# Two weight tensors laid out ahead of four work tensors in SBUF, in a two-layer graph kernel

## The chip, the cores and the metric

The kernel runs on one core of one Trainium2 chip. The metric is the device time of one execution, in microseconds (us); lower is better. The time before is the median of three runs.

## The reference

128 graphs of 128 nodes with 256 features go through two layers. The first is a layer norm, a ReLU, a linear layer and a product with a weighted adjacency matrix, with a residual. The second is a layer norm, a ReLU, graph attention with 8 heads, an output projection, a sigmoid and a residual.

```python
h = jnp.maximum(_layernorm(x, axis=-1), 0.0)
x = x + (adj @ (h @ L0_weight) + L0_bias)
h = jnp.maximum(_layernorm(x, axis=-1), 0.0)
feat_proj = (h @ fc_w + fc_b)                  # 8 heads of 256 columns
logits = feat_proj @ q_w + q_b + swap(feat_proj @ k_w + k_b)
attn = softmax(leaky_relu(logits + (1.0 - adj) * NEG, 0.01))
out = concat_heads(attn @ feat_proj) @ fp_w + fp_b + h
x = x + sigmoid(out)
```

All data is float32.

## The kernel before

Nodes lie on the 128 partitions. Two graphs make a pair (`j` is 0 or 1 in it), and there are 64 pairs. The kernel first multiplies each head's `fc_w` by its rows of `fp_w`, so that one 256 by 256 matrix per head is left; the eight are kept as `m_hi` and `m_lo`, the rounded values and what the rounding left over (`fold`, with its matmuls on line 417). Precision is kept in the whole kernel in this way: an operand is split in a high and a low part of type float32r, and `split` (line 396) makes a product of three matmuls, low by high, high by low and high by high.

For each pair, TensorE does this. A matmul has a stationary operand, which a weight load brings into the array, and a moving operand, which streams through it.

- `aggregate` (line 442): adjacency by features, float32, with `h0_f` stationary and `g_in` moving. In the profile: `bank<-g_in,h_f`.
- `transform`: `ah_hi`, `ah_lo` stationary, the first layer's weights `w0_hi`, `w0_lo` moving, 256 columns. In the profile: `bank<-w_hi,ah_lo` and the like.
- `transpose_h` (line 465), and `queries_keys` (line 478) with `u` stationary and `hT_hi`, `hT_lo` moving, 256 columns.
- `project`, 8 calls of 6 matmuls: `hT_hi`, `hT_lo` stationary, `m_hi`, `m_lo` moving, 512 columns. In the profile: `gbank<-m_hi,hT_lo` and the like. ScalarE copies each bank to `g_hi[j]` (line 1249), and VectorE subtracts that from the bank to give `g_lo[j]` (line 830).
- `transpose_p` (line 497), after which ScalarE and VectorE write `pT_hi[j]` (line 1263) and `pT_lo[j]` (line 837).
- `attend`, 4 calls of 12 matmuls: `pT_hi[j]`, `pT_lo[j]` stationary, `g_hi[j]`, `g_lo[j]` moving, 256 columns. In the profile: `ybank<-g_hi,pT_lo` and the like.

The work of neighbouring pairs overlaps. The order of the work on each of the five engines is written out by hand: a beginning, a loop whose body `step` handles one pair (57 passes on TensorE), and an end. Semaphores join the engines.

What the change touches is the allocation of SBUF at the head of `gnn_pair`. `sb(name, shape, dt, align)` takes the next free bytes of every partition, from the next multiple of `align`; `two(...)` makes two tensors, one for each `j`. `LINE` is 64 bytes and `SPAN` 256. `ah`, `hT`, `pT`, `fcb` and `m` are placed at multiples of `SPAN`, `w0`, `g` and `u` at multiples of `LINE`. `fcb` is 64 bytes long. A row of `m` is `MROW` = 576 elements, and `project` reads its 512 columns from element `MAT` = 16, so 64 bytes into the row. The loops, the semaphores and the tensors' sizes say nothing of addresses.

Of the kernel before, what the change touches and what calls it, by code (L numbers as in the profile page):

```python
# [6 lines left out]
F32R = mybir.dt.float32r  # L7
# [3 lines left out]
P = 128  # L11
D = 256
DT = D // P
# [16 lines left out]
SPAN = 256  # L30


HP = H // 2
MAT = LINE // 4
MROW = 2 * D + 64
# [15 lines left out]
def gnn_pair(nc, graph, identity, head_mask, row_coef, w0, bias0, fc_wT, fc_b, qk_w, q_b, k_b, fp_w, fp_b, out):  # L51
# [9 lines left out]
    with ExitStack() as ctx:  # L61
        def sb(name, shape, dt=F32, align=32):
            return ctx.enter_context(nc.sbuf_tensor(name, shape, dt, align_bytes=align))
# [7 lines left out]
        def two(name, shape, dt=F32, align=32):  # L71

            return [sb(f"{name}{k}", shape, dt, align) for k in range(J)]
# [13 lines left out]

        fcb = sb("fcb", [P, H * DT], F32, SPAN)
        w0_hi, w0_lo = sb("w0_hi", [P, DT, D], F32R, LINE), sb("w0_lo", [P, DT, D], F32R, LINE)
        g_hi, g_lo = two("g_hi", [P, H * D], F32R, LINE), two("g_lo", [P, H * D], F32R, LINE)  # L90

        u = sb("u", [P, DT, 2 * HALF], F32R, LINE)
        m_hi, m_lo = sb("m_hi", [P, DT, HP, MROW], F32R, SPAN), sb("m_lo", [P, DT, HP, MROW], F32R, SPAN)


        ident = sb("ident", [P, P])
# [1793 lines left out]
```

How the kernel before makes its waits and increments, by code:

```python
            def load(p, q):  # L253
                if has(p - U):
                    sp.wait_ge(a_h0f, 2 * (p - U + 1))
                    sp.wait_ge(pe_ah, p - U + 1)
                    sp.wait_ge(g_xb, p - U + 1)
                    sp.wait_ge(g_t, p - U + 1)
                if has(p - 1):
                    sp.wait_ge(s_loaded, 16 * (p + 1) - 16)
                sp.dma_start(g_in[q][:], graph[p]).then_inc(s_loaded, 16)
# [1 line left out]
            def store(p):  # L263
                sp.wait_ge(g_res, p + 1)
                sp.dma_start(out[p].rearrange("n (j d) -> n j d", j=J), res).then_inc(s_stored, 16)
# [1 line left out]
            def keys_out(p, q):  # L267
                sp.wait_ge(v_kq, p + 1)
                if has(p - 1):
                    sp.wait_ge(s_rows, 16 * p)
                sp.dma_start(key_rows[q][0:HALF + ROWS], kq_sb[q][0:HALF + ROWS]).then_inc(s_rows, 16)
# [1 line left out]
            def queries_in(p, q):  # L273
                sp.wait_ge(s_rows, 16 * (p + 1))
                if has(p - 1):
                    sp.wait_ge(s_queries[0], 16 * p)
                    sp.wait_ge(s_queries[1], 16 * p)
                if has(p - U):
                    for n in range(J * NC):
                        sp.wait_ge(v_mx[n], p - U + 1)
                for j in range(J):
                    rows = key_rows[q][j * HALF + H:j * HALF + ROWS].rearrange("h n -> n h")
                    sp.dma_start(qs[q][:, j, :], rows, allow_slow_non_contiguous=True).then_inc(s_queries[j], 16)
```

## Time and profile before

| | |
|---|---|
| median of three runs | 1412.72 us (1412.06 to 1412.76) |
| profiled execution, its own time | 1412.72 us |
| its span, first to last instruction | 1410.8 us |
| granted TensorE clock, mean over the span | 0.999 |
| TensorE matmul busy | 1400.5 us, 99% |
| weight load busy | 1258.8 us, 89% |
| VectorE / ScalarE / GpSimd busy | 1286.0 / 1125.6 / 1102.2 us |

The span leaves out 1.9 us of the profiled execution's time. Busy time of TensorE is not a measure of its pace here: matmuls are pipelined, their ends are modelled, and one that is shown with 0.28 us is followed by the next after 0.11 us. The pace is read from the starts in the timeline.

### The profile page before, as it was taken

To read this page: it belongs to the slowest core of one execution; us is meant where nothing else is said; L and a number is where in the kernel's file an instruction comes from. 1 tells how busy PE (TensorE), PEld (TensorE's weight loads), DVE (VectorE), ACT (ScalarE), POOL (GpSimd) and SP (SyncE) were. 2 spreads that over 40 slices of the span, in tenths; PEclk is the share of its full clock that TensorE was granted. 3 is DMA by queue.
4 is the path that set the end of the run, shared out by engine and by line. 5 is a ranking of instruction groups with operands and counts; after the bars stand their busy time and mean duration, and the time that the engine had idled before them with its cause. 6 is when DMAs were issued, how large, how long until landed. Compare 5 with 4: busy or idle time off the path is not lost.

```text
span 1410.8 us, 31568 instructions
## 1 busy us (share of the span) xinstructions
PE 1400.5 (99%) x9048; PEld 1258.8 (89%) x9048; DVE 1286.0 (91%) x4396; ACT 1125.6 (80%) x3417; POOL 1102.2 (78%) x1297
## 2 busy tenths in 40 slices
PE   9999999999999999999999999999999999999998
PEld 7888999899899899998998998998989989988987
DVE  7999999999999999999999999999999999998996
ACT  4878788788888888887887888888878878887876
POOL 5787877878778878778787787787787877878764
PEclk9999999999999999999999999999999999999999
DMA  7323323323223233233132232232331332322321
GB/s 240 94 63 107 107 54 105 95 65 105 78 81 106 58 101 106 54 105 100 59 105 82 77 106 61 98 106 54 105 103 56 105 85 74 106 66 85 76 58 42
DMA packets 177131, 124.68 MB, mean 88 GB/s; under 512 B 137808, under 2 KB 143568, under 8 KB 177104
## 3 DMA queue, kind: packets, MB, share of 16 engines
q1 hardware_dynamic: 176816, 124.35, 30.4%
q8 instruction: 12, 0.20, 0.1%
q14 instruction: 15, 0.12, 0.0%
q10 hardware_dynamic: 288, 0.01, 0.0%
HBM read 105.98 MB, written 18.35 MB: 88 GB/s over the span
## 4 chain that ended last, share of the span: by engine, by line
PE 94%; POOL 2%; DMA 1%; issue 1%; DVE 1%; SPq 0%; ACT 0%; POOLq 0%
PE gbank L396 48%; PE ybank L396 24%; PE tbank L497 8%; PE bank L396 6%; PE bank L442 4%; PE bank L478 2%; PE bank L465 2%; DMA late<-fc_wT_dram 1%; PE gbank L417 1%; DMA late<-key_rows 0%; POOL att L1587 0%; POOL att L1580 0%; DVE att L847 0%; POOL ends L1603 0%; DVE att L854 0%
## 5 line engine op out<-in xcount | busy, mean ns | idle before, releaser
L1256 ACT ACTIVATE att<-att 128x128 f32<-128x128 f32 x1024 | 397.8, 393 | 43.3 <-DVE att L854 39.2
L1580 POOL TENSOR_TENSOR att<-late,t_pos 128x512 f32<-128x512 f32 x256 | 330.6, 1293 | 127.9 <-PE tbank L497 122.7
L396 PE MATMUL gbank<-m_hi,hT_lo 128*128 128x512 f32 x1024 | 428.0, 418 | 0.0
L396 PE MATMUL gbank<-m_hi,hT_hi 128*128 128x512 f32 x1024 | 402.0, 393 | 0.0
L396 PE MATMUL gbank<-m_lo,hT_hi 128*128 128x512 f32 x1024 | 401.5, 392 | 0.0
L830 DVE TENSOR_TENSOR g_lo<-gbank,g_hi 128x512 fp32r<-128x512 f32 x512 | 341.5, 679 | 47.5 <-ACT g_hi L1249 42.9
L1587 POOL TENSOR_TENSOR att<-att,rinv 128x512 f32<-128x512 f32 x256 | 288.9, 1129 | 106.8 <-DVE rinv L859 106.4
L1249 ACT ACTIVATE g_hi<-gbank 128x512 fp32r<-128x512 f32 x512 | 290.6, 594 | 42.5 <-PE gbank L396 42.2
L847 DVE TENSOR_SCALAR_CACHE_REDUCE att<-att,qs 128x128 f32<-128x128 f32 x1024 | 291.7, 341 | 30.4 <-POOL att L1580 30.1
L396 PE MATMUL ybank<-g_hi,pT_lo 128*128 128x256 f32 x1016 | 283.2, 279 | 0.0
L396 PE MATMUL ybank<-g_hi,pT_hi 128*128 128x256 f32 x1016 | 283.0, 279 | 0.0
L396 PE MATMUL ybank<-g_lo,pT_hi 128*128 128x256 f32 x1016 | 282.5, 278 | 0.0
L1263 ACT ACTIVATE pT_hi<-tbank 128x512 fp32r<-128x512 f32 x256 | 152.9, 597 | 149.0 <-PE tbank L497 144.1
L396 PEld LDWEIGHTS gbank<-m_hi,hT_hi 128*128 128x128 f32 x1024 | 192.2, 188 | 43.3
L396 PEld LDWEIGHTS gbank<-m_lo,hT_hi 128*128 128x128 f32 x1024 | 193.7, 189 | 25.1
L396 PEld LDWEIGHTS gbank<-m_hi,hT_lo 128*128 128x128 f32 x1024 | 192.9, 188 | 25.5
L396 PEld LDWEIGHTS ybank<-g_lo,pT_hi 128*128 128x128 f32 x1016 | 190.8, 188 | 10.4
L396 PEld LDWEIGHTS ybank<-g_hi,pT_lo 128*128 128x128 f32 x1016 | 190.9, 188 | 9.9 <-DVE pT_lo L837 0.2
L1256 ACT ACTIVATION_READ_ACCUMULATOR att<-att 128x1 f32 x1024 | 194.8, 190 | 0.0
L854 DVE SCALAR_TENSOR_TENSOR att<-att 128x516 f32<-128x516 f32 x256 | 193.8, 775 | 0.2
L396 PEld LDWEIGHTS ybank<-g_hi,pT_hi 128*128 128x128 f32 x1016 | 190.5, 187 | 0.0
L837 DVE TENSOR_TENSOR pT_lo<-tbank,pT_hi 128x512 fp32r<-128x512 f32 x256 | 173.7, 678 | 5.3 <-ACT pT_hi L1263 4.3
(97 smaller groups left out, 2317.9 us busy)
## 6 DMA issues: line engine op xcount, KB each, us to landing
late<-key_rows SPq DMA_DIRECT2D x64, 1024.0 KB, 6.1
g_in<-graph_dram SPq DMA_DIRECT2D x64, 512.0 KB, 3.4
out_dram<-ends SPq DMA_DIRECT2D x63, 256.0 KB, 3.8
qs<-key_rows SPq DMA_DIRECT2D x128, 4.0 KB, 2.4
key_rows<-kq_sb SPq DMA_DIRECT2D x64, 24.0 KB, 1.4
att<-fc_wT_dram SPq DMA_DIRECT2D x4, 256.0 KB, 5.7
late<-fp_w_dram SPq DMA_DIRECT2D x4, 256.0 KB, 5.3
ends<-fp_w_dram SPq DMA_DIRECT2D x2, 512.0 KB, 7.8
```

The costliest lines, as they stand in the source:

```text
L396: mm = pe.matmul(out_ap, w, m, start=first and n == 0, stop=last and n == len(terms) - 1)
L442: mm = pe.matmul(sums[:, j, dt, :], h0_f[q][:, j, dt * P:(dt + 1) * P], adjT_of(q)[:, j, :], start=True, stop=True)
L497: mm = pe.transpose(tbank[:, h * P:(h + 1) * P], att[j][c][:, h * P:(h + 1) * P], ident[:])
L830: dve.tensor_tensor(g_lo[j][:, s], bank[:], g_hi[j][:, s].bitcast(F32), ALU.subtract)\
L837: dve.tensor_tensor(pT_lo[j][:, hs, :], rows, pT_hi[j][:, hs, :].bitcast(F32), ALU.subtract)\
L847: r = dve.tensor_scalar(a[:, s], a[:, s], qs[q][:, j, c * HC + h:c * HC + h + 1], None, ALU.add, ALU.min, accum_out=a[:, CH + h:CH + h + 1])
L854: dve.scalar_tensor_tensor(out=a, in0=a, scalar=SLOPE, in1=a, op0=ALU.mult, op1=ALU.min)\
L1249: act.activation(g_hi[j][:, s], gbank[tenant(RING, RSIZE, n, p)[0]][:], ACT.Copy).then_inc(a_g[n], 1)
L1256: e = act.activation(a[:, s], a[:, s], ACT.Exp, scale=-1.0, bias=a[:, CH + h:CH + h + 1], accum_out=esum[j][c][:, h:h + 1])
L1263: act.activation(pT_hi[j][:, c * HC:(c + 1) * HC, :], rows, ACT.Copy).then_inc(a_pT[NC * j + c], 1)
L1580: gp.tensor_tensor(a, keys[q][:, j, c * HC:(c + 1) * HC, :], t_pos[q][:, j, :].unsqueeze(1).broadcast_to([P, HC, P]), ALU.add)\
L1587: gp.tensor_tensor(a, a, rinv[j][c][:].unsqueeze(2).broadcast_to([P, HC, P]), ALU.mult)\
```

## The change

The line that allocates `m_hi` and `m_lo` moves up, from behind `u` to before `g_hi` and `g_lo`. Nothing else is changed.

```diff
@@ -87,10 +87,10 @@
 
         fcb = sb("fcb", [P, H * DT], F32, SPAN)
         w0_hi, w0_lo = sb("w0_hi", [P, DT, D], F32R, LINE), sb("w0_lo", [P, DT, D], F32R, LINE)
+        m_hi, m_lo = sb("m_hi", [P, DT, HP, MROW], F32R, SPAN), sb("m_lo", [P, DT, HP, MROW], F32R, SPAN)
         g_hi, g_lo = two("g_hi", [P, H * D], F32R, LINE), two("g_lo", [P, H * D], F32R, LINE)
 
         u = sb("u", [P, DT, 2 * HALF], F32R, LINE)
-        m_hi, m_lo = sb("m_hi", [P, DT, HP, MROW], F32R, SPAN), sb("m_lo", [P, DT, HP, MROW], F32R, SPAN)
```

Each engine executes the same instructions in the same order, with the same waits. The addresses follow from the sizes and alignments; the first aligned tensor starts at byte 16640 of a partition.

| tensor | start before | mod 256 | start after | mod 256 |
|---|---|---|---|---|
| `pT_hi0`, `pT_hi1`, `pT_lo0`, `pT_lo1` | 41216, 45312, 49408, 53504 | 0 | the same | 0 |
| `w0_hi`, `w0_lo` | 57664, 59712 | 64 | the same | 64 |
| `g_hi0`, `g_hi1` | 61760, 69952 | 64 | 98816, 107008 | 0 |
| `g_lo0`, `g_lo1` | 78144, 86336 | 64 | 115200, 123392 | 0 |
| `u` | 94528 | 64 | 131584 | 0 |
| `m_hi`, `m_lo` | 95232, 113664 | 0 | 61952, 80384 | 0 |
| `ident`, and all behind it | 132096 | 0 | the same | 0 |

The 192 bytes that padding takes ahead of `m_hi` are taken in both kernels, so nothing behind `m` or `u` moves. The columns of `m` that `project` reads start at 64 mod 256 in both. `hT` and `ah` lie at 0 mod 256 and stay where they are.

## Rows read from the trace of the kernel before

**Rows 1.** The page: span, TensorE's busy time and granted clock in 40 slices, the chain by engine.
```profile
span 1410.8 us, 31568 instructions
...
PE 1400.5 (99%) x9048; PEld 1258.8 (89%) x9048; DVE 1286.0 (91%) x4396; ACT 1125.6 (80%) x3417; POOL 1102.2 (78%) x1297
...
PEclk9999999999999999999999999999999999999999
...
PE 94%; POOL 2%; DMA 1%; issue 1%; DVE 1%; SPq 0%; ACT 0%; POOLq 0%
```
**Rows 2.** Waits of TensorE in 60:1350: line, waited for: us, times, longest.
```profile
PE bank L465 <- ACT h L1233: 0.8, 1, 0.8
PE tbank L497 <- POOL att L1587: 0.5, 1, 0.5
```
**Rows 3.** The chain that ended last: start us, length us; one place, two passes.
```profile
707.54 2.76 PE gbank L396 x12
729.07 2.76 PE gbank L396 x12
```
**Rows 4.** Timeline of TensorE, `attend` with `g1`, `pT1`: start us, us.
```profile
702.84 0.28 PE L396 MATMUL ybank<-g_hi,pT_lo 128*128 128x256 f32 x1
702.95 0.28 PE L396 MATMUL ybank<-g_lo,pT_hi 128*128 128x256 f32 x1
...
704.20 0.39 PE L396 MATMUL gbank<-m_hi,hT_lo 128*128 128x512 f32 x1
```
**Rows 5.** The same, `attend` with `g0`, `pT0`.
```profile
713.33 0.28 PE L396 MATMUL ybank<-g_hi,pT_lo 128*128 128x256 f32 x1
713.45 0.28 PE L396 MATMUL ybank<-g_lo,pT_hi 128*128 128x256 f32 x1
...
714.75 1.06 PE L442 MATMUL bank<-g_in,h_f 128*128 128x128 f32 x8
715.64 0.60 PE L497 MATMUL tbank<-ident,att 128*128 128x128 f32 x4
```
**Rows 6.** The same, one early `attend` with `g0`, `pT0`: first and last start.
```profile
113.59 0.28 PE L396 MATMUL ybank<-g_hi,pT_lo 128*128 128x256 f32 x1
...
114.84 0.28 PE L396 MATMUL ybank<-g_hi,pT_hi 128*128 128x256 f32 x1
```
**Rows 7.** The same, one early `attend` with `g1`, `pT1`: first and last start.
```profile
79.49 0.28 PE L396 MATMUL ybank<-g_hi,pT_lo 128*128 128x256 f32 x1
...
80.79 0.28 PE L396 MATMUL ybank<-g_hi,pT_hi 128*128 128x256 f32 x1
```
**Rows 8.** Timeline of TensorE, `queries_keys` of pair 0 and of a later pair.
```profile
27.56 0.28 PE L478 MATMUL bank<-hT_hi,u 128*64 128x256 f32 x1
27.67 0.28 PE L478 MATMUL bank<-hT_lo,u 128*64 128x256 f32 x1
27.78 0.28 PE L478 MATMUL bank<-hT_hi,u 128*64 128x256 f32 x1
...
700.99 0.28 PE L478 MATMUL bank<-hT_lo,u 128*64 128x256 f32 x1
701.46 0.39 PE L396 MATMUL gbank<-m_hi,hT_lo 128*128 128x512 f32 x1
```
**Rows 9.** Timeline of TensorE, 12 matmuls of `fold` in the beginning, and three of them.
```profile
11.32 2.78 PE L417 MATMUL gbank<-late,att 128*128 128x258 f32 x12
...
11.98 0.82 PE L417 MATMUL gbank<-late,att 128*128 128x258 f32 x3
```
**Rows 10.** Groups by line: shapes xcount | busy us, mean ns | idle before.
```profile
L830 DVE TENSOR_TENSOR g_lo<-gbank,g_hi 128x512 fp32r<-128x512 f32 x512 | 341.5, 679 | 47.5 <-ACT g_hi L1249 42.9
L837 DVE TENSOR_TENSOR pT_lo<-tbank,pT_hi 128x512 fp32r<-128x512 f32 x256 | 173.7, 678 | 5.3 <-ACT pT_hi L1263 4.3
L1249 ACT ACTIVATE g_hi<-gbank 128x512 fp32r<-128x512 f32 x512 | 290.6, 594 | 42.5 <-PE gbank L396 42.2
L1263 ACT ACTIVATE pT_hi<-tbank 128x512 fp32r<-128x512 f32 x256 | 152.9, 597 | 149.0 <-PE tbank L497 144.1
```
**Rows 11.** Busy time of the engines in the stretch 60:1350.
```profile
60.00:1350.00 1290.00, 1288.68 (x8373) 1160.44 (x8372) 1189.13 (x4072) 1045.00 (x3169) 1032.37 (x1198) 1.00 0.30 85
```

## The prediction

> **What bounds the kernel now.** I read four views in this order. The page comes first: TensorE is busy for 1400.5 of 1410.8 us, its clock is granted in full in every slice (2.4 GHz), and no other engine is above 91% [rows 1]. A busy share does not prove a bound, since the ends of matmuls are modelled. So the waits come second: between 60 and 1350 us, which is 91% of the span, TensorE's instructions waited for other engines twice, 1.3 us in all [rows 2]. The chain of waits says the same in another way: one place of the loop comes back after 729.07 - 707.54 = 21.53 us, and 94% of the chain is TensorE's [rows 1, 3]. The loop's 57 passes are then 57 x 21.53 = 1227 us, and their length is the sum of TensorE's own steps. The timeline comes last, because it shows those steps. What a reader is to see there is the distance between starts, not the duration.
>
> In an `attend` on the second graph, 12 matmuls of 256 columns take 704.20 - 702.84 = 1.36 us, 0.113 us each [rows 4]. In one on the first graph they take 714.75 - 713.33 = 1.42 us, 0.118 each [rows 5]. 256 columns at one per cycle of 2.4 GHz would be 0.107 us, so both are above the bare columns. Call the two paces quick and slow. Going through the starts of all 256 calls of `attend` in the trace, I count 121 quick (4 on `g0`, 117 on `g1`) and 135 slow (124 and 11).
>
> **The change part by part.** No instruction, wait or transfer is added, removed or reordered on any engine. What changes are addresses: `m` starts 33,280 bytes lower, and `g` and `u` start 37,056 bytes higher. So there are three things that could carry a time.
>
> *1. The residue of `g` under TensorE's reads.* `g` goes from 64 to 0 mod 256, and becomes equal there to `pT`, the weights loaded beside it. This concerns 256 x 12 = 3072 matmuls, and as nothing covers TensorE, each nanosecond on each of them is 3.1 us of the end. No float32r stretch of this trace has both operands at the same residue, so the cost has to be bounded.
> - If the pace hung on which addresses meet, `g0` and `g1` would differ always. They don't: the usually slow `g0` runs quick at 113.59, with 11 steps in 114.84 - 113.59 = 1.25 us, 0.114 each [rows 6], and the usually quick `g1` runs slow at 79.49, with 1.30 / 11 = 0.118 [rows 7]. Same tensors, same addresses, both paces. What differs is what stood ahead and how the stream came in. This is the strongest thing that the trace says for an address-free pace.
> - `queries_keys` has the mirrored residues, 0 moving and 64 stationary. In pair 0 its starts are 27.56, 27.67, 27.78, 0.11 apart: quick. Later its four take 701.46 - 700.99 = 0.47, 0.118 each: slow [rows 8]. The mirrored pair knows the same two paces.
> - Equal residues do occur in float32, at half the column rate. `aggregate` has both operands at 224 mod 256: its 8 records start over 715.64 - 714.75 = 0.89 us, 0.111 each, 0.0046 above the 256 cycles (0.1067) of its columns [rows 5]. `fold` has its weights at 96 and the moving operand at 32 to 240. The 12 records of [rows 9] have it at 72, 88, 96 and 112, four of them at 96, equal. The 12 cover 2.78 us; less the last one's 0.38 that is 2.40 / 11 = 0.218, 0.003 above the 516 cycles (0.215) of their columns, and the three that start at 11.98, of which the last two are equal ones, cover 0.82, so (0.82 - 0.38) / 2 = 0.22 each as well. No price of equality is seen there. `aggregate`'s excess over `fold`'s, 0.0046 - 0.003, less than 0.002 us for 512 bytes read, would be 0.004 for the 1024 bytes of a `g` matmul. I don't take it, since the two differ in shape too, but it is the upper end: 3072 x 0.004 = 12.3 us.
> - The lower end is that every slow call turns quick: 135 x (1.42 - 1.36) = 8.1 us gained.
> I take 0, by the nearest rows, [rows 6 to 8], which are the same type and the same width, and keep -8.1 and +12.3.
>
> The page "SBUF — State Buffer" of the Trainium skill, section "Who interferes with whom", gives TensorE two independent SBUF read ports, one for the moving operand and one for weight loads, and says that it never waits on anyone. By this rule the sum is 0 exactly. The trace agrees only in part: 0.113 and 0.118 against 0.107 show that something beside the columns costs time, and the rule does not name it, so it does not close the range.
>
> *2. The residue of `u`, and the absolute place of `m` and `g`.* `u` moves onto `hT`'s residue, in 4 x 64 = 256 matmuls. Between its two paces of 0.113 and 0.118 that is at most 256 x 0.005 = 1.3 us either way; I take 0. The columns read from `m` stay at 64 mod 256. Its row starts step by 2304 bytes and `g`'s by 1024 under `pT`'s 512, so the higher address bits already take many combinations inside one call, and the step within a call stays the same to 0.01 us [rows 4, 5]. A large boundary, such as 65536, already lies inside `g_hi0` before. I take 0 for the place.
>
> *3. The other engines' reads and writes of `g`.* VectorE writes `g_lo` at residue 64 in 679 ns and `pT_lo` at residue 0 in 678. ScalarE writes `g_hi` in 594 and `pT_hi` in 597 [rows 10]. So the residue is worth 3 ns at most. That is also off the path: VectorE is busy for 1189 of 1290 us in the steady stretch [rows 11], so it has about 100 us of room over some 480 writes of `g_lo` there, 0.2 us for each, before TensorE would have to wait for it. I take 0.
>
> The sum is 0. From the profiled execution: span 1410.8 + 0, with the 1.9 us that lie around it, gives 1412.7 us, which is also the median of the runs shown.
>
> **The rivals.**
> *Slower: equal residues lock `attend` into the slow pace.* The place is the moving read of `g` beside the load of `pT`. If reads that start on the same residue get in each other's way, the 121 quick calls become slow: 121 x 0.06 = 7.3 us, and the time is 1420.0. It decides from 1 ns a matmul upwards (3.1 us). For it: all float32r streams that are quick have the two operands at different residues, and `aggregate`, with equal ones, has a larger excess than `fold`. Against it: both paces on the same addresses [rows 6, 7], and equal residues at no price in `fold` [rows 9]. With the 0.004 of the upper end instead it would be 1425.0.
>
> *Faster: the slow calls turn quick.* The pace depends on how the stream before came in, so a small shift anywhere, an altered step in `queries_keys` or in `m`, can tip the calls on `g0`, 124 slow ones of 128, into the quick pace: up to 124 x 0.06 = 7.4 us with `g0` alone, 1405.3. For it: it needs only a nudge, and such calls exist [rows 6]. Against it: if addresses don't enter at all, nothing nudges, and the loop repeats as before.
>
> *The projection shifts instead.* `project` has 64 x 48 = 3072 matmuls of 512 columns. If its steps moved by 0.002 us on the average, that would be 6 us, to either side. Nothing in its residues changes, so this would have to be passed on from `attend`; I count it with the two above.
>
> **How the numbers follow.** A measurement of this kernel can tell about 0.2% from no change, 2.8 us. No effect of addresses, or one below that: 0.60. The slower rival, whole or in part: 0.25. The faster one: 0.15. The predicted time is that of the likeliest case, 1412.7. Its own range is 1411.5 to 1414. To leave out no more than 2 in 10 the range takes in the slower rival's 1420.0 and most of the faster rival: 1406 to 1420.5.
>
> **What would show it right or wrong.** Right: the place of [rows 3] still returns after 21.53 us, `attend` still has its 1.36 and 1.42 us calls in the same places, and the writes of `g` keep 679 and 594 ns. The slower rival shows as 1.42 us or more in `attend` on the second graph, with no wait of TensorE for another engine. The faster one shows as 1.36 us on the first graph. A wait of TensorE for VectorE's `g_lo` in the steady stretch would prove step 3 wrong. The forecast falls if a pass of the loop is longer or shorter than 21.53 by more than 0.05 us, for 57 of those are 2.8 us.

## The result, and the profile after

The changed kernel takes 1425.53 us (median, 1425.15 to 1426.06), the kernel before 1412.39 us in the same comparison. The ratio is 1.0094, with a 95% interval of 1.0077 to 1.0111: slower by 13.1 us. No change was forecast, and the time lies outside the stated range.

The page of the changed kernel, and the waits of TensorE in 60:1350, beside [rows 1] and [rows 2]:
```profile
span 1423.7 us, 31568 instructions
...
PE 1414.5 (99%) x9048; PEld 1271.2 (89%) x9048; DVE 1286.5 (90%) x4396; ACT 1124.1 (79%) x3417; POOL 1101.4 (77%) x1297
...
PEclk9999999999999999999999999999999999999999
```
```profile
PE tbank L497 <- POOL att L1587: 0.5, 1, 0.5
PE bank L465 <- ACT h L1233: 0.3, 1, 0.3
```
TensorE's clock is granted in full as before and it still waits for nobody (0.8 us). The busy times of the other engines are the same within 1.5 us. So the 12.9 us of span arise on TensorE itself. The chain of waits shows the length of a pass of the loop, as in [rows 3] (start us, length us):
```profile
496.30 2.76 PE gbank L396 x12
518.04 2.76 PE gbank L396 x12
```
A pass is now 21.74 us, 0.21 more than 21.53, and 57 x 0.21 = 12.0 of the 12.9 us. Note that the 12 `project` matmuls in the row still take 2.76 us. The timeline shows which ones don't. First a call of `attend` on `g1`, `pT1`, to be held against the 1.36 us of [rows 4]:
```profile
708.84 0.28 PE L396 MATMUL ybank<-g_hi,pT_lo 128*128 128x256 f32 x1
708.96 0.28 PE L396 MATMUL ybank<-g_lo,pT_hi 128*128 128x256 f32 x1
709.08 0.28 PE L396 MATMUL ybank<-g_hi,pT_hi 128*128 128x256 f32 x1
...
710.28 0.40 PE L396 MATMUL gbank<-m_hi,hT_lo 128*128 128x512 f32 x1
```
Then one on `g0`, `pT0`, to be held against the 1.42 us of [rows 5]:
```profile
719.50 0.28 PE L396 MATMUL ybank<-g_hi,pT_lo 128*128 128x256 f32 x1
...
720.94 0.27 PE L442 MATMUL bank<-g_in,h_f 128*128 128x128 f32 x1
```
Both take 1.44 us, 0.120 a matmul. The quick pace of 0.113 is gone, and what was slow (0.118) is a little slower. The groups by line show the same on their own scale. The modelled duration of a matmul of `attend` went from 279 to 283 ns, while that of `project` stays at 393, and the writes of `g` by VectorE and ScalarE stay where [rows 10] had them. First two groups of the kernel before, then the changed kernel:
```profile
L396 PE MATMUL gbank<-m_hi,hT_hi 128*128 128x512 f32 x1024 | 402.0, 393 | 0.0
...
L396 PE MATMUL ybank<-g_hi,pT_hi 128*128 128x256 f32 x1016 | 283.0, 279 | 0.0
```
```profile
L396 PE MATMUL gbank<-m_hi,hT_hi 128*128 128x512 f32 x1024 | 402.2, 393 | 0.0
L830 DVE TENSOR_TENSOR g_lo<-gbank,g_hi 128x512 fp32r<-128x512 f32 x512 | 341.4, 678 | 47.7 <-ACT g_hi L1249 43.0
L1249 ACT ACTIVATE g_hi<-gbank 128x512 fp32r<-128x512 f32 x512 | 290.6, 594 | 49.6 <-PE gbank L396 49.3
...
L396 PE MATMUL ybank<-g_hi,pT_hi 128*128 128x256 f32 x1016 | 287.8, 283 | 0.0
```

For the whole execution I summed the distances from each matmul's start to the next, by what it reads:

| us of the chain on TensorE | `attend` on g0 | `attend` on g1 | `project` | `transform` | `queries_keys` |
|---|---|---|---|---|---|
| before | 182.5 | 175.7 | 734.5 | 88.8 | 30.5 |
| after | 184.6 | 184.5 | 736.5 | 88.8 | 30.3 |
| difference | +2.1 | +8.8 | +2.0 | 0.0 | -0.2 |

### The profile page after: what moved, and what is told of

Its sections match the earlier page's. It is cut to its first block, busy times and chain, and to the rows that moved or that the text cites. A ratio compares the mean times of both kernels' runs of the same rounds, so it can differ in the third digit from the quotient of the medians.

```text
span 1423.7 us, 31568 instructions
## 1 busy us (share of the span) xinstructions
PE 1414.5 (99%) x9048; PEld 1271.2 (89%) x9048; DVE 1286.5 (90%) x4396; ACT 1124.1 (79%) x3417; POOL 1101.4 (77%) x1297
## 4 chain that ended last, share of the span: by engine, by line
PE 94%; POOL 2%; DVE 1%; issue 1%; DMA 1%; ACT 0%; POOLq 0%; SPq 0%; ACTq 0%
PE gbank L396 48%; PE ybank L396 25%; PE tbank L497 8%; PE bank L396 6%; PE bank L442 4%; PE bank L478 2%; PE bank L465 2%; DMA late<-key_rows 0%; POOL att L1587 0%; POOL att L1580 0%; DMA qk<-qk_w_dram 0%; PE gbank L417 0%; DVE att L847 0%; POOL xb L1570 0%; POOL t_pos L1572 0%
## 5 line engine op out<-in xcount | busy, mean ns | idle before, releaser
L396 PE MATMUL ybank<-g_hi,pT_hi 128*128 128x256 f32 x1016 | 287.8, 283 | 0.0
L396 PE MATMUL ybank<-g_lo,pT_hi 128*128 128x256 f32 x1016 | 287.3, 283 | 0.0
L396 PE MATMUL ybank<-g_hi,pT_lo 128*128 128x256 f32 x1016 | 287.2, 283 | 0.0
```

The source lines that it names most:

```text
L396: mm = pe.matmul(out_ap, w, m, start=first and n == 0, stop=last and n == len(terms) - 1)
```

## The experiments

The theory after the result: a float32r matmul is slower when its moving operand and the weights that are loaded beside it start at the same address mod 256 (the same residue). Rivals: the absolute place of `m` or `g` in the partition; a bad start at 0 mod 256 in itself; and `u`, which moved too. In what follows "distance" is the moving operand's start less the weights' start, mod 256. In every experiment each engine's instructions and waits are the same, in the same order; only addresses differ. Where a kernel says `ident` with `SPAN`, all that lies behind moves by 256 bytes or (in `e8_m_0`) not at all, so it keeps its residues.

**Place or residue.** `e1_place` is the changed kernel with 64 bytes ahead of `g`:
```diff
+        gap0 = sb("gap0", [P, 16], F32, LINE)
         g_hi, g_lo = two("g_hi", [P, H * D], F32R, LINE), two("g_lo", [P, H * D], F32R, LINE)
-        ident = sb("ident", [P, P])
+        ident = sb("ident", [P, P], F32, SPAN)
```


> m stays ahead of g as in the changed kernel, but g and u start 64 bytes later, so both are again at 64 mod 256; ident and all behind it move by 256 bytes, which keeps their residues. If the residue of g (or u) costs the 13 us, this is as fast as the kernel before: 1412 to 1414, with attend calls of 1.36 and 1.42 us. If the absolute place of m or g costs them, it stays at 1425, with calls of about 1.44 us.

Measured: 1412.82 us, ratio to before 1.0002 (0.9992 to 1.0012). With `m` ahead of `g`, but `g` back at 64, all of the loss is gone. Its call on `g1` in the timeline:
```profile
703.29 0.28 PE L396 MATMUL ybank<-g_hi,pT_lo 128*128 128x256 f32 x1
...
704.65 0.39 PE L396 MATMUL gbank<-m_hi,hT_lo 128*128 128x512 f32 x1
```
1.36 us, as in [rows 4]. `e2_g_u_0` is the reverse: the order of before, `m` on its old bytes, `g` and `u` at 0.
```diff
-        g_hi, g_lo = two("g_hi", [P, H * D], F32R, LINE), two("g_lo", [P, H * D], F32R, LINE)
+        g_hi, g_lo = two("g_hi", [P, H * D], F32R, SPAN), two("g_lo", [P, H * D], F32R, LINE)
```


> The order of before, m at its old bytes, g and u moved up by 192 bytes to 0 mod 256 into the padding ahead of m; nothing else moves. Residue theory: 1424 to 1427, attend calls of about 1.44 us. Place theory: 1412 to 1414.

Measured: 1424.63 us, ratio 1.0084 (1.0067 to 1.0101), a pass of 21.74 us. The loss is back without the move of `m`. The two together show that the place costs nothing and the residue all. `e1_place` also says something of the period: there `g` starts 320 bytes past `pT` mod 512, in the kernel before 64 bytes, and the time is the same.

**`g` or `u`.** `e3_u_0` gives `u` the alignment `SPAN` in the kernel before; `f0_g_0` puts `g` at 0 and keeps `u` at 64.
```diff
-        u = sb("u", [P, DT, 2 * HALF], F32R, LINE)
+        u = sb("u", [P, DT, 2 * HALF], F32R, SPAN)
```

> The kernel before with u alone at 0 mod 256 (moved up by 192 bytes); g, m and all else at their bytes. If only g's residue matters: 1412.4 within 1 us, attend unchanged. If u's share is what tips the pace of the whole loop: most of the 13 us.

> g alone at 0 mod 256, u kept at 64 (m and all behind it 256 bytes higher, residues kept). If g's equality with pT makes the whole of the 12 us: 1423 to 1426, attend near 120 ns in every call. If it needs u at 0 too: about 1420, since u alone gave 4.3 us.

Measured: `f0_g_0` 1426.1 us, ratio 1.0092 (1.0075 to 1.0108). A call on `g1` takes 1.44 us:
```profile
709.19 0.28 PE L396 MATMUL ybank<-g_hi,pT_lo 128*128 128x256 f32 x1
...
710.63 0.40 PE L396 MATMUL gbank<-m_hi,hT_lo 128*128 128x512 f32 x1
```
So `g` alone makes the whole loss, and `u` adds nothing to it. `e3_u_0` gave 1416.97 us, 1.0029 (1.0018 to 1.0041), where I had expected no change. Its own `queries_keys` got no slower (30.2 us against 30.5), although its operands are now at distance 0. So the theory does not hold for that stream, whose four matmuls at a time have only 64 columns of weights. But other calls changed their pace. On `g0` it is quick now (first two rows), on `g1` slow (last two):
```profile
716.12 0.28 PE L396 MATMUL ybank<-g_hi,pT_lo 128*128 128x256 f32 x1
...
717.49 0.27 PE L442 MATMUL bank<-g_in,h_f 128*128 128x128 f32 x1
```
```profile
705.47 0.28 PE L396 MATMUL ybank<-g_hi,pT_lo 128*128 128x256 f32 x1
...
706.88 0.40 PE L396 MATMUL gbank<-m_hi,hT_lo 128*128 128x512 f32 x1
```
1.37 us and 1.41 us. Summed over the execution: g0 -6.1, g1 +5.9, `transform` +2.8, `project` +1.6, which is +4.2 us.

**Equality, or a start at 0.** `e4_both_64` moves `pT` to 64, so that `g` and `pT` are equal at 64; `e5_mirror` has `pT` at 64 and `g` at 0 (`u` stands ahead of `g` in it, still at 64).
```diff
-        pT_hi, pT_lo = two("pT_hi", [P, H, P], F32R, SPAN), two("pT_lo", [P, H, P], F32R, SPAN)
+        gap0 = sb("gap0", [P, 16], F32, LINE)
+        pT_hi, pT_lo = two("pT_hi", [P, H, P], F32R, LINE), two("pT_lo", [P, H, P], F32R, LINE)
```


> pT moves by 64 bytes to 64 mod 256, g stays at 64 (all from pT on at the same residue as before, 256 bytes higher, but pT at 64). If it is the equality of the moving operand's and the loaded weights' residues that costs: 1422 to 1427. If it is g's own start at 0 mod 256: 1412 to 1414.

> The kernel before with pT at 64 mod 256 and g at 0 mod 256: the residues differ again, but g starts where it does in the changed kernel. u stays at 64, m and w0 keep their residues. Equality theory: near the kernel before, 1410 to 1418 (the pace of the calls may be dealt out otherwise), attend at 113 to 118 ns a matmul. Theory that g must not start at 0 mod 256: 1422 to 1427, about 120 ns.

Measured: `e4_both_64` 1423.97 us, 1.008 (1.0063 to 1.0097); `e5_mirror` 1416.3 us, 1.0025 (1.0015 to 1.0035). A call on `g1` in `e4_both_64`, then in `e5_mirror`:
```profile
708.02 0.28 PE L396 MATMUL ybank<-g_hi,pT_lo 128*128 128x256 f32 x1
...
709.47 0.40 PE L396 MATMUL gbank<-m_hi,hT_lo 128*128 128x512 f32 x1
```
```profile
703.88 0.28 PE L396 MATMUL ybank<-g_hi,pT_lo 128*128 128x256 f32 x1
...
705.26 0.39 PE L396 MATMUL gbank<-m_hi,hT_lo 128*128 128x512 f32 x1
```
1.45 us with `g` on the very residue it has before, and 1.38 with `g` on the residue of the changed kernel. Summed over the execution, `attend` takes 357.9 us in `e5_mirror` and 358.2 in the kernel before. Most of the 3.5 us that `e5_mirror` loses lie in `transform` (+3.0), which was entered by 228 to 230 ns instead of 231 or 232 in nearly all calls (more on that below). Equality costs, not the start at 0.

**Other distances.** `e6_g_128` and `e7_g_192` put gaps of 64 and 128 bytes ahead of `g` and keep `u` at 64.
```diff
+        gap0 = sb("gap0", [P, 16], F32, LINE)   # 32 elements in the other
         g_hi, g_lo = two("g_hi", [P, H * D], F32R, LINE), two("g_lo", [P, H * D], F32R, LINE)
+        gap1 = sb("gap1", [P, 48], F32, LINE)   # 32 in the other
         u = sb("u", [P, DT, 2 * HALF], F32R, LINE)
```

> g at 128 mod 256, pT at 0, u at 64, all behind m moved by 256 bytes. If only equal residues cost: 1408 to 1418, attend at 113 to 118 ns. If the cost falls with the distance of the residues: below 1411. If the distance of 64 bytes ahead is the only good one: about 1425.

> g at 192 mod 256, the rest as with 128. Equality theory: 1408 to 1418. If the two reads walk through the same four 64-byte lines with the weights' read behind or ahead, 192 (which is 64 the other way round) may cost as much as 0: 1418 to 1427.

Measured: 1421.85 us, 1.0063 (1.0046 to 1.008), and 1418.55 us, 1.0038 (1.0024 to 1.0052). I had hoped for gains at one or the other; both lose, and 1421.85 lies outside all three cases that I had written down for it. The mean distance between starts in `attend`, over 30 pairs of the loop in each trace, g0 and g1 taken together:

| distance | kernels | ns a matmul |
|---|---|---|
| 64 | `h1`, `h2` (below); before, `e1`, `e3`; `f1` (below) | 113.7; 115.9; 118.0 |
| 192 | `e5_mirror`, `e7_g_192` | 116.1, 117.7 |
| 128 | `e6_g_128` | 118.9 |
| 0 | after, `e2_g_u_0`, `e4_both_64`, `f0_g_0` | 119.5 to 119.9 |

At 64 the mean is a mixture of the two paces, and ranges with it; the kernels with `g` at 64 that the table leaves out lie between its ends (`f3` and `h3` near 115.9, `f2` 117.0, `e8`, below, 117.9). At 0 and 128 every kernel's mean is above even the slow pace. At 192 the quick pace turns up in part of a call; throughout it stood in one call of the 512 in the two traces.

**`project` at distance 0.** `e8_m_0` moves `m` to 192 mod 256, so that the columns read from it start at 0, as `hT` does.
```diff
-        m_hi, m_lo = sb("m_hi", [P, DT, HP, MROW], F32R, SPAN), sb("m_lo", [P, DT, HP, MROW], F32R, SPAN)
+        gap0 = sb("gap0", [P, 32], F32, LINE)
+        m_hi, m_lo = sb("m_hi", [P, DT, HP, MROW], F32R, LINE), sb("m_lo", [P, DT, HP, MROW], F32R, LINE)
```

> The kernel before with m 192 bytes past a multiple of 256, so that the columns which project reads start at 0 mod 256 as hT does; g and u untouched. Equality theory: the 3072 matmuls of project cost more too, by 2 to 6 ns each: 1418 to 1431, with attend unchanged. If only calls of 256 columns are hit, because there the weight load takes up all of the matmul's time: 1412 to 1415.

Measured: 1422.58 us, 1.007 (1.0054 to 1.0087), in the range expected but not for the reason. `project` itself took 735.6 us, 1.1 more, or 0.4 ns a matmul. Equality has no price of its own there that shows: `e3_u_0` and `f2_u_192` spent 1.6 and 1.9 more in `project` with `m` at 64. What rose is what stands behind it: g1 +6.1, `transform` +2.8, as both are at 118 ns throughout.

**How the pace is handed on.** `f1_u_128` and `f2_u_192` move `u` alone; `f3_ident_64` moves `ident` and all that lies behind it by 64 bytes, and with it the float32 operands of the transposes and of `aggregate`, all together.
```diff
+        gap0 = sb("gap0", [P, 16], F32, LINE)   # ahead of u in f1 (32 elements in f2), ahead of ident in f3
```

> u alone at 128 mod 256, nothing else moves. queries_keys itself is 30.5 us in all and can change by 1 us. If u acts through what it hands on to the calls behind it (as with u at 0, where g0 turned quick and g1 and transform slow), the time goes anywhere from 1406 to 1419, by which calls run at 113 and which at 118 ns; without that, 1412 to 1414.

> u alone at 192 mod 256, nothing else moves. Same reasoning: 1406 to 1419 if the handing on differs, 1412 to 1414 if it does not. In both cases every call of attend has all its matmuls at either 113 or 118 ns, never at 120.

> g, u and m untouched; ident and all tensors behind it (att, h1, h0_f, g_in among them) 64 bytes higher, so the float32 transposes and aggregate read from other residues. If float32 streams don't care about residues: 1412 to 1414. If they hand on another start to project, the paces are dealt out anew: 1406 to 1420.

Measured: `f1_u_128` 1421.23 us, 1.0057 (1.004 to 1.0074), above the expected 1419: nearly all calls of `attend` and `transform` were at 118 ns. `f2_u_192` 1418.03 us, 1.0033 (1.0021 to 1.0046), with one of the two calls on g1 slow. `f3_ident_64` 1413.5 us, 1.0002 (0.9992 to 1.0011). As all float32 operands moved together there, their distances from each other stayed, so that run is one more for the place being worth nothing, and says nothing on equal residues in float32. In all three each call was at 113 or at 118, as expected, but for a step or two at its start.

These traces hold a rule. Take the last matmul of `project` ahead of a call of `attend`, and the distance from its start to the next start. In the nine kernels that have both `g` and `m`'s columns at distance 64 (before, `e1`, `e3`, `f1` to `f3`, and the three below), 231 or 232 ns there came ahead of 1106 calls, and every one was quick. Any other value (225 to 230, 233 and above) came ahead of 1081 calls, and every one was slow. (13 calls of `attend` in each kernel stand behind another stream than `project` and are not counted.) That step ends with the call's first start, so it might be the first sign of the pace only. But the step before it, between the last two matmuls of `project`, is over before the call begins, and it sorts the calls as well: 229 or 230 ns ahead of all 1106 quick ones, 225, 226 or 231 to 234 ahead of all 1081 slow ones.

In those of the nine kernels that have `w0` at distance 64, `transform` follows the rule of 231 or 232 too, but for one early call, where the step of 429 ns holds a wait and a quick call follows. Outside the nine it is not strict: 233 ns came ahead of eight quick calls of `transform` in `e2_g_u_0` and `e6_g_128`, and 231 ahead of a slow one in `e8_m_0`. So the pace of a call is foretold by how TensorE comes out of `project`. And a change of `u`'s residue alone changed those steps and dealt the paces out anew. That the way in is what causes the pace is argued from this; no run changed it by itself.

**Does it hold for `w0`, and can all of `attend` be quick?** `h1_w0_0`, `h2_w0_128` and `h3_w0_192` put a gap of 192, 64 or 128 bytes ahead of `w0` and another behind it, so that `g` stays at 64.
```diff
+        gap0 = sb("gap0", [P, 48], F32, LINE)   # 16 and 32 elements in the other two
         w0_hi, w0_lo = sb("w0_hi", [P, DT, D], F32R, LINE), sb("w0_lo", [P, DT, D], F32R, LINE)
+        gap1 = sb("gap1", [P, 16], F32, LINE)   # 48 and 32
         g_hi, g_lo = two("g_hi", [P, H * D], F32R, LINE), two("g_lo", [P, H * D], F32R, LINE)
```


> w0 at 0 mod 256, equal to ah; g and u at 64 as before (all from g on 256 bytes higher). Equality theory: transform goes from 113.8 to about 120 ns a matmul, 768 x 6 = 4.7 us. If g0's pace follows from how transform ended (with u at 0 transform was slow and g0 quick), g0 turns quick and gives back 6 us: 1410 to 1413. If it does not: 1416 to 1419.

> w0 at 128 mod 256, ah at 0. By the distances seen on g, transform runs at about 119 ns, 4 us more. With g0 quick: 1409 to 1412; without: 1415 to 1418.

> w0 at 192 mod 256, ah at 0. By the distances seen on g, transform runs at about 117.6 ns, 3 us more. With g0 quick: 1408 to 1411, faster than both kernels; without: 1414 to 1417.

Measured: 1412.31 us, 0.9996 (0.9987 to 1.0006); 1411.28 us, 0.9988 (0.9978 to 0.9997); 1415.54 us, 1.0019 (1.0009 to 1.0028). `transform` went from 113.8 to 119.9, 118.9 and 118.2 ns, though it was entered by 231 or 232 ns in nearly all calls of all three, which at distance 64 made it quick: about the cost by distance of `attend`, in another stream. In the first two g0 turned quick as well (176.5 and 176.3 us against 182.5), in the third it did not. `h2_w0_128`, `transform` and then the call on g0:
```profile
709.25 0.28 PE L396 MATMUL bank<-w_hi,ah_lo 128*128 128x256 f32 x1
...
710.68 0.27 PE L497 MATMUL tbank<-ident,att 128*128 128x128 f32 x1
```
```profile
712.51 0.28 PE L396 MATMUL ybank<-g_hi,pT_lo 128*128 128x256 f32 x1
...
713.87 0.27 PE L442 MATMUL bank<-g_in,h_f 128*128 128x128 f32 x1
```
1.43 us and 1.36 us. `h2_w0_128` is 1.7 us faster than the kernel before and the fastest of all, though by little more than the measurement can tell, and it gets there by a slower `transform`. A layout with `transform` and all of `attend` quick was not found.

## Why the prediction was wrong

- **The bound** was read right. TensorE alone sets the time, 21.53 us a pass before and 21.74 after, without waits in both.
- **Step 1 failed: the residue of `g` was costed at nothing.** It costs 10.9 us in `attend` (+2.1 on g0, +8.8 on g1) and 2.0 more in `project` behind it, 12.9 of span. The 2.0 need not be equality's own, since `f2_u_192`, with `g` at 64, has 1.9 of it. The upper end that I kept, 12.3 us from the excess of `aggregate`, came near the measured loss, but whether equal residues make that excess was not tried, so this may be chance. I put the end into the working and then cut the range at 1420.5.
- **The argument that failed** was "same tensors, same addresses, both paces", hence an address-free pace. Its facts stand [rows 6, 7]: the call at 113.59 was entered by 231 ns, the one at 79.49 by 229, as the rule says. But it shows only that something beside the addresses sets the pace. It does not show that addresses don't. Both do: the distance decides which paces a stream can take (113 or 118 at 64; 120 on the average at 0), and the way in goes with which of them it takes.
- **The mirrored pair** (`queries_keys`) and `fold` [rows 8, 9] were read as evidence that residues have no price. The mirrored pair has unequal residues, so it said nothing about equal ones, and `fold` takes columns at half the rate in float32. What I read from `fold` stands: its steps are 0.217 to 0.220 us with equal and unequal residues alike. The trace of before held no float32r stream with equal residues, as the working said, and 0.60 for no effect was too much for a case that no row showed.
- **The slower rival** had the right place and sign, and the relation that the runs bear out, equal residues. Its price was 7.3 us, as if equality could only lock the slow pace of 0.118; the changed kernel has 0.120 and hands on 2.0 us to `project`.
- **The faster rival's mechanism is real.** A change of other residues does deal the paces out anew (`e3`, `f1`, `f2`, `h1`, `h2`). Of these only `h1` and `h2` did not lose.
- **Steps 2 and 3 held in what the change did.** The place of `m` and `g` is worth nothing (`e1_place`), VectorE's and ScalarE's writes kept 678 and 594 ns, and `u`'s move added nothing to `g`'s (`f0_g_0` against `e2_g_u_0`, 1.0092 and 1.0084, intervals that overlap). By itself `u` would have cost 4.3 us, more than my 1.3: I had bounded its own matmuls, which got no slower, and not what it hands on.
- The page "SBUF — State Buffer" of the Trainium skill, section "Who interferes with whom", calls TensorE's two SBUF read ports independent and says that TensorE never waits on anyone. I had made of that a sum of exactly 0. These runs don't bear that out: `attend`'s matmuls follow each other after 119.5 to 119.9 ns at distance 0 and after 113.7 at their best, and in the changed kernel TensorE waited for other engines for 0.8 us only. Whether the reads meet in the memory, in the array or in what feeds it, no run here shows.

What stays open is why 231 or 232 ns is the step that goes with the quick pace, and why neither `project` nor `queries_keys` gets slower itself at distance 0.

## What to carry to other kernels

When TensorE is the bound and streams narrow float32r matmuls with a weight load for each, the start addresses of the moving operand and of the weights are a parameter worth a percent: in `attend` and `transform` here the moving operand 64 bytes past the weights mod 256 was best and equality worst, while `queries_keys` and `project` did not slow down themselves. Check it after every change in the order of allocations. Read the pace from the distances of starts in the timeline, call by call, because two kernels with the same instructions can differ there and nowhere else. And a case that no row of the trace covers calls for a range that holds both ends of its bound, however good the argument for one of them looks.

## What the runs showed of the hardware

- The distance mod 256 between the moving operand and the weights changes the pace of float32r matmuls of 256 columns: 113.7 to 118.0 ns at 64, 116.1 to 117.7 at 192, 118.9 at 128, 119.5 to 119.9 at 0, in `attend`. `transform`, entered in the same way, gives 113.8, 118.2, 118.9 and 119.9 for the same four. It is not so for every stream: at distance 0 the matmuls of `queries_keys` (64 columns of weights) took 30.2 us in all against 30.5 (`e3_u_0`), and those of `project` (512 columns moving) 735.6 against 734.5 (`e8_m_0`).
- TensorE's steps repeat within a nanosecond or two and carry a state. At distance 64 a stream of such matmuls keeps its 113 or 118 ns to its end, and the last step of `project` ahead of it (231 or 232 ns, or another) foretold which in all 2187 calls of `attend` that stand right behind `project`, in nine kernels.
- Where the tensors lie beyond their residues is worth nothing here: `m` 33 KB lower and `g` 37 KB higher gave 1.0002 (0.9992 to 1.0012), all float32 tensors 64 bytes on gave 1.0002 (0.9992 to 1.0011).
